# Layer 1 of a two-layer transformer kernel: the values of four heads by Strassen's seven products, with other homes for weights, queries and outputs

## What is computed

```
q = (x @ wq).reshape(B, S, 32, 192)[..., :128]
k = (x @ wkv)[..., :4096].reshape(B, S, 32, 128)
v = (x @ wkv)[..., 4096:8192].reshape(B, S, 32, 128)
probs = softmax(where(causal, q k^T * 192**-0.5, -1e30))
x = layernorm(x + (probs @ v).reshape(B, S, 4096) @ wo)
```

## Time and profile before

| | |
|---|---|
| time, median of 3 runs | 1414.67 us (1414.52 to 1414.96) |
| the profiled execution | 1416.18 us |
| its span, first to last instruction | 1414.4 us |
| TensorE busy | 1399.7 us (99%) |
| VectorE, ScalarE, GpSimd busy | 1015.6, 891.3, 773.7 us |
| layer 1's attention | from about 488 to 1340 us of the span |

### The profile page before, as it was taken

One profiled execution on the slowest core, in us unless ns is written; L12 is line 12 of the kernel. 1 busy time (PEld: TensorE's weight loads), 2 busy tenths in 40 slices (PEclk: granted clock), 3 DMA queues, 4 the chain that ended last, 5 costly groups with the idle time before them and its releaser, 6 DMA issues.

```text
span 1414.4 us, 30207 instructions
## 1 busy us (share of the span) xinstructions
PE 1399.7 (99%) x8769; PEld 1236.1 (87%) x8769; DVE 1015.6 (72%) x2528; ACT 891.3 (63%) x2445; POOL 773.7 (55%) x828
## 2 busy tenths in 40 slices
PE   9999999999999999999999999999999999999998
PEld 7898989888788888889889889889889889889886
DVE  5999999998968875665665665665665665665776
ACT  5888888888555576566566566566566556556721
POOL 3645555555040367765665665665665665665521
PEclk9999999999999999999999999999999999999999
DMA  5533333322445301111001002001001001000201
GB/s 197 164 100 89 101 89 100 89 73 50 129 139 155 107 31 46 46 31 59 30 30 59 30 30 59 30 30 59 30 30 59 30 30 59 30 30 30 83 20 42
DMA packets 56155, 92.60 MB, mean 65 GB/s; under 512 B 6064, under 2 KB 27312, under 8 KB 56112
## 3 DMA queue, kind: packets, MB, share of 16 engines
q1 hardware_dynamic: 55968, 91.93, 21.7%
q10 hardware_dynamic: 144, 0.13, 0.0%
HBM read 81.82 MB, written 2.10 MB: 59 GB/s over the span
## 4 chain that ended last, share of the span: by engine, by line
PE 93%; DVE 3%; ACT 2%; issue 1%; POOL 1%; DMA 0%; SPq 0%; POOLq 0%; DVEq 0%; ACTq 0%
PE c_bv L106 8%; PE c_bv L108 7%; PE c_bv L107 7%; PE h_bo L947 5%; PE c_bx L106 5%; PE c_bx L108 4%; PE c_bx L107 4%; PE c_by L106 4%; PE c_by L108 4%; PE c_by L107 4%; PE h_bo L1450 3%; PE a_acc L1450 3%; PE h_bt L75 3%; PE c_bt L75 2%; PE h_bs L106 2%; PE h_bs L108 2%
## 5 line engine op out<-in xcount | busy, mean ns | idle before, releaser
L621 POOL TENSOR_TENSOR h_pr<-h_pr,h_rinv 128x512 f32<-128x512 f32 x128 | 133.2, 1041 | 136.8 <-DVE h_rinv L772 134.5
L1781 POOL TENSOR_TENSOR c_qk<-g_y,c_qk 128x512 fp32r<-128x512 f32 x96 | 124.1, 1293 | 146.1 <-ACT c_qk L1893 139.3
L1632 POOL TENSOR_TENSOR b_sw_lo<-b_slots,b_sw_hi 128x512 fp32r<-128x512 f32 (+1 forms) x128 | 148.0, 1156 | 10.3
L1630 POOL CAST b_sw_hi<-b_slots 128x512 fp32r<-128x512 f32 (+1 forms) x128 | 72.7, 568 | 143.9 <-DMA b_slots<-in_w_qk 120.8
L106 PE MATMUL c_bv<-b_wv_hi,g_xT_hi 128*128 128x256 f32 x496 | 138.9, 280 | 0.2 <-DVE g_xT_lo L1186 0.2
L107 PE MATMUL c_bv<-b_wv_lo,g_xT_hi 128*128 128x256 f32 x496 | 138.8, 280 | 0.0
L108 PE MATMUL c_bv<-b_wv_hi,g_xT_lo 128*128 128x256 f32 x496 | 138.7, 280 | 0.0
L2002 DVE TENSOR_TENSOR c_bo<-c_bo,g_wo 128x128 f32<-128x128 f32 x128 | 38.3, 299 | 122.0 <-ACT g_wo L1868 117.5
L1893 ACT ACTIVATE c_qk<-g_y 128x512 fp32r<-128x512 f32 x96 | 60.7, 632 | 96.8 <-DVE g_y L2039 67.3
L674 ACT ACTIVATE h_pr<-h_bs,h_nmax 128x256 f32<-128x256 f32 x256 | 119.4, 480 | 2.5 <-DVE h_nmax L767 2.4
L1858 ACT ACTIVATE c_pr<-c_pr,c_rinv 128x128 f32<-128x128 f32 (+1 forms) x256 | 101.9, 448 | 9.0 <-DVE c_rinv L1992 9.0
(11 more groups left out here) (480 smaller groups left out, 5139.5 us busy)
## 6 DMA issues: line engine op xcount, KB each, us to landing
f_wi<-in_w_ffn SPq DMA_DIRECT2D x66, 256.0 KB, 2.7
b_slots<-in_w_qk SPq DMA_DIRECT2D x64, 256.0 KB, 3.0
a_w<-in_w_head SPq DMA_DIRECT2D x28, 352.0 KB, 2.9
h_part<-in_w_ffn SPq DMA_DIRECT2D x32, 264.0 KB, 2.8
b_raw_v<-in_w_v SPq DMA_DIRECT2D x16, 512.0 KB, 4.6
b_raw_o<-in_w_o SPq DMA_DIRECT2D x16, 512.0 KB, 4.5
h_o_mix<-h_o_hi SPq DMA_DIRECT2D x62, 128.0 KB, 2.2
b_ffn_w<-in_w_ffn SPq DMA_DIRECT2D x4, 576.0 KB, 5.5
```

Source lines behind the costliest of these rows:

```text
L621: pool.tensor_tensor(pr[b][:, :, :], pr[b][:, :, :], rinv[b][:, :][:, :, None].to_broadcast([P, 2, S]), ALU.mult)\
L1632: pool.tensor_tensor(self.sw[1][:, a:b], self.slots[:, a:b], f32(self.sw[0][:, a:b]), ALU.subtract)\
L1781: pool.tensor_tensor(lo, src, f32(hi), ALU.subtract).then_inc(s_sumlo, 1)
```

## The change

The unit of the loop is a quad `q` of four heads j with 16 steps u = 4j + t; quads 1 to 6 are the loop.

- Values of a quad are made by Strassen's scheme on two by two blocks: weights of 256 channels x 256 columns (two heads), tokens in halves of 512 and channels in halves of 256, worked on for one batch of each token half at a time ("pair" 0 and 1). `value_product` is 12 matmuls of 256 columns. The seven products v1 to v7 stand at u = 12 (v1, v2), 13 (v6, v5), 14 (v7), 15 (v4, v3) for pair 0; v1 of pair 1 comes at the end of u = 15, and v2, v6, v5, v7, v4, v3 at u = 0 to 2 of the quad itself. They gather in bv and a new bank bw. ScalarE copies bv (`value_copy`), VectorE adds bw (`value_total`), and four "corners" of v are split by ScalarE (`corner_hi`) and VectorE (`corner_lo`): 11, 22 and 12 from the summed copies in SBUF (`vy`), 21 from the bank bv. The first quad has straight values as before (`straight_batch`).
- GpSimd makes four sums of value weights per quad (`combine_v`, 128x512 each) and splits seven blocks (`split_v`) in place of 1024 columns per group.
- Outputs: one bank bo, so `values(s)` waits for `outs` of step s-1 (before: s-2). The outputs of heads go to three homes, and a fourth for the last head; the output weights lie in v's own home (even pairs) or in an unused part of xT (odd pairs). Tiles of the odd pair 2q-1 stand at u = 3 to 7 (2, 1, 2, 1, 2), of the even pair 2q at u = 8 to 11, and alternate between bv and bw.
- Queries and keys: one buffer. `sum_hi` 1 and 2 both stand at t = 2 (before: t = 1 and 2), and GpSimd's `rest` 1 and 2 follow split 2.
- SyncE loads the output weights when their home is free (`load_o`), the value weights of a quad in three transfers (`load_v`). The scratch that the program reserves for dynamic transfers is set to 256.

The diff, cut to its core:

```diff
+    def combine_v(self, pool, q):
+        lo, a21 = self.vraw[1], self.vraw[0][:, self.VS4, :]
+        def put(out, a, b, op):
+            pool.tensor_tensor(lo[:, out, :], a, b, op).then_inc(self.s_vhi, 1)
+        done = 11 * q - 9
+        pool.wait_ge(self.s_in["v"], 48 * q + 32)
+        put(self.VS1, a21, lo[:, self.VA22, :], ALU.add)
+        put(self.VS3, lo[:, self.VA11, :], a21, ALU.subtract)
+        pool.wait_ge(self.s_vhi, done + 1)
+        put(self.VS2, lo[:, self.VS1, :], lo[:, self.VA11, :], ALU.subtract)
+        pool.wait_ge(self.s_vhi, done + 3)
+        put(self.VS4, lo[:, self.VA12, :], lo[:, self.VS2, :], ALU.subtract)
+        pool.wait_ge(self.s_vhi, done + 4)
...
-        qk = [k.sb(f"qk{i}", [P, 2, 2, T], F32R) for i in range(2)]
...
+        qk = k.sb("qk", [P, 2, 2, T], F32R)
...
-        bo = [k.ps(f"bo{i}") for i in range(2)]
+        bw, bo = k.ps("bw"), k.ps("bo")
...
                 if now:
-                    rest(h + 1, 0, q0)
+                    rest(h + 1, 0)
                 if more and not entry:
                     self.combine(pool, h + 2)
-                if hd == 0 and has(gr + 1, NG):
-                    self.split(pool, "v", gr + 1, [(s_vmm, 4 * gr + 4)])
-                if hd == 1 and has(gr, NG - 1):
-                    if isinstance(gr, int) and gr == 0:
-                        pool.wait_ge(s_tslo, 4)
-                    self.split(pool, "o", gr, [(s_omm, 8 * gr)])
+                if ahead and j >= 2:
+                    for i in ((0, 1, 2), (5, 6))[j - 2]:
+                        self.split_v(pool, q + 1, i)
                 if more:
                     self.split_qk(pool, h + 2, 1, [(s_x, 4 * h + 6), (s_y, 3 * h + 4)])
+                    self.split_qk(pool, h + 2, 2, [(s_x, 4 * h + 7), (s_y, 3 * h + 5)])
+                if ahead and j == 2:
+                    for i in (3, 4):
+                        self.split_v(pool, q + 1, i)
                 if now:
-                    rest(h + 1, 1, k1)
-                if more:
-                    self.split_qk(pool, h + 2, 2, [(s_x, 4 * h + 7), (s_y, 3 * h + 5)])
-                if now:
-                    rest(h + 1, 2, q1)
+                    rest(h + 1, 1)
+                    rest(h + 1, 2)
                 if more:
                     self.split_qk(pool, h + 2, 3, [(s_x, 4 * h + 8), (s_y, 3 * h + 6)])
-                if hd == 0 and in_last(gr):
-                    self.split(pool, "o", gr, [(s_wlo, 4 * NH)])
+                if entry:
+                    return
+                if j == 1:
+                    self.split_o(pool, 2 * q, wo_homes[0])
+                    if ahead:
+                        self.combine_v(pool, q + 1)
+                if j == (2 if is_last(q) else 3):
+                    self.split_o(pool, 2 * q + 1, wo_homes[1])
...
+                    b = straight_batch(q, u - 1)
+                    if b is not None:
+                        value_hi(NB + b, 1, b, tile_bank(b))
+                    if filled and u == 0:
+                        value_copy(2 * q - 1, 0)
+                    if filled and u == 1:
+                        corner_hi(2 * q - 1, "11", 1)
+                    if filled and u == 2:
+                        value_copy(2 * q - 1, 2)
+                    if filling and u == 13:
+                        corner_hi(2 * q, "11", 0)
+                    if filling and u == 15:
+                        corner_hi(2 * q, "22", 0)
+                    probs(s)
                     if has(s - 1, NSTEP):
-                        outs(s - 1, hd if t else 1 - hd, (t - 1) % 4)
-                    keys_first = light(gr, hd) and t == 2
+                        outs(s - 1, out_region(h - 1 if t == 0 else h, (j - 1) % 4 if t == 0 else j), (t - 1) % 4)
+                    if filled and u == 0:
+                        corner_hi(2 * q - 2, "12", 0)
+                    if filled and u == 1:
+                        value_copy(2 * q - 1, 1)
+                    if filled and u == 3:
+                        corner_hi(2 * q - 1, "12", 1)
+                    keys_first = light(h) and t == 2
                     if keys_first:
-                        key_hi(h + 1, 1 - hd)
+                        key_hi(h + 1)
                     if has(s + 1, NSTEP):
                         exps(s + 1, (t + 1) % 4)
+                    if filling and u == 12:
+                        value_copy(2 * q, 0)
+                    if filling and u == 13:
+                        value_copy(2 * q, 1)
                     if t < 2 and has(h + 1, NH):
                         copy(h + 1, t + 1)
                     if t == 2 and has(h + 1, NH) and not keys_first:
-                        key_hi(h + 1, 1 - hd)
+                        key_hi(h + 1)
+                    if filling and u == 14:
+                        value_copy(2 * q, 2)
+                    if filling and u == 15:
+                        corner_hi(2 * q, "21", 0)
                     if has(s + 1, NSTEP):
                         normalise(s + 1, (t + 1) % 4)
                     if t == 3 and has(h + 2, NH):
                         copy(h + 2, 0)
-                    if t < 3 and has(h + 1, NH):
-                        sum_hi(h + 1, 1 - hd, t)
-                    if hd == 1 and in_last(gr):
+                    if t == 0 and has(h + 1, NH):
+                        sum_hi(h + 1, 0)
+                    if t == 2 and has(h + 1, NH):
+                        sum_hi(h + 1, 1)
+                        sum_hi(h + 1, 2)
+                    if filled and u == 2:
+                        corner_hi(2 * q - 1, "22", 1)
+                        corner_hi(2 * q - 1, "21", 1)
...
+                    b = straight_batch(q, u - 1)
+                    if b is not None:
+                        value_lo(NB + b, 1, b, tile_bank(b))
+                    if filled and u == 0:
+                        value_total(2 * q - 2, 2)
+                    if filled and u == 1:
+                        corner_lo(2 * q - 1, "11", 1)
+                    if filled and u == 3:
+                        value_total(2 * q - 1, 2)
+                    if filling and u == 13:
+                        corner_lo(2 * q, "11", 0)
+                    if filling and u == 15:
+                        corner_lo(2 * q, "22", 0)
                     if has(s + 1, NSTEP):
                         maxes(s + 1, (t + 1) % 4)
-                    few = light(gr, hd)
+                    few = light(h)
                     if few and t == 3:
                         probs(s)
                     if has(s - 1, NSTEP):
-                        outs(s - 1, hd if t else 1 - hd, (t - 1) % 4)
-                    if has(s, NSTEP) and not (few and t == 3):
+                        outs(s - 1, out_region(h - 1 if t == 0 else h, (j - 1) % 4 if t == 0 else j), (t - 1) % 4)
+                    if not (few and t == 3):
                         probs(s)
+                    if filled and u == 0:
+                        corner_lo(2 * q - 2, "12", 0)
+                    if filled and u == 3:
+                        corner_lo(2 * q - 1, "12", 1)
                     if few and t == 2:
-                        key_lo(h + 1, 1 - hd)
+                        key_lo(h + 1)
                     if has(s + 1, NSTEP):
                         inverse(s + 1, (t + 1) % 4)
-                    if hd == 0 and not in_last(gr) and has(gr - 1, NG):
-                        add_out(8 * (gr - 1) + 2 * t, 2 * t, bv)
+                    add(0)
+                    if filled and u == 2:
+                        value_total(2 * q - 1, 1)
                     if t == 2 and has(h + 1, NH) and not few:
-                        key_lo(h + 1, 1 - hd)
+                        key_lo(h + 1)
+                    if filled and u == 0:
+                        value_total(2 * q - 1, 0)
+                    if filling and u == 12:
+                        value_total(2 * q, 0)
                     if t < 3 and has(h + 1, NH):
                         total(h + 1, t)
-                    if hd == 0 and not in_last(gr) and has(gr - 1, NG):
-                        add_out(8 * (gr - 1) + 2 * t + 1, 2 * t + 1, bv if t < 3 else by)
-                    if in_last(gr):
-                        steps = last_steps.get((hd, t), ())
-                        if hd == 1 and t == 2:
+                    add(1)
+                    if filling and u == 14:
+                        value_total(2 * q, 1)
+                    if filling and u == 15:
+                        corner_lo(2 * q, "21", 0)
+                    if filled and u == 2:
+                        corner_lo(2 * q - 1, "22", 1)
+                        corner_lo(2 * q - 1, "21", 1)
...
+                def v1(to, pair):
+                    n = 2 * to - 2 + pair
+                    if pair:
+                        pe.wait_ge(s_clo, corners(n - 1, "21"))
+                    else:
+                        pe.wait_ge(s_oadd, 16 * to - 9)
```

(72 more changed lines are left out.)

504 lines of the change are left out of this document (311 added, 193 removed).

## The result

The median after is 1419.5 us (1417.87 to 1420.64, 7 runs), before in the same session 1414.96 us (1414.52 to 1416.15, 7 runs): a ratio of 1.0031, 95% interval 1.0021 to 1.0041. The profiled execution took 1418.15 us with a span of 1416.2, against 1416.18 and 1414.4.

What follows compares the result with a forecast made beforehand. TensorE was taken to bound layer 1 without waits; -19.9 us of matmuls plus 9.8, 7.7 and 2.0 us of new waits gave -0.4 us, so 1414.3 us. The range was 1403 to 1422 us, the forecast's own 1411 to 1418.

Steps and rivals of the forecast that it cites:

- What bounds the kernel, and the price of a product: TensorE bounds layer 1; 14 blocks of 12 matmuls replace 16 in seven quads, at 1.42 us each: 19.9 us saved.
- Rival 3: Something beside TensorE's work limits the loop, so time follows the new waits only: 1425 us and more; chance 0.04.
- (a): One bank for outputs: values waits for the split of the step before; nothing, up to 0.3 us in steps without tiles.
- (b): One buffer of queries and keys, sum_hi 1 and 2 both at t = 2: costs nothing.
- (f): GpSimd's added combinations and half-blocks: 81 us of about 104 per quad, a queue costing nothing, with 0.8 us cover.
- (g): Six more 512-column operations per quad on ScalarE and VectorE, 3.6 us, falling into idle time, and the loads: nothing.
- rival 2: GpSimd's queue arrives late at u = 12, 1.0 us in seven quads: 1421 us; chance 0.22.
- (c): Hand-over at u = 2 to 3: first output tile waits for corner_lo 21 of pair 1, 1.4 us in seven quads: 9.8 us.
- (d): Hand-over at u = 15: v1 of pair 1 waits for corner_lo 21 of pair 0, 1.1 us seven times: 7.7 us.
- (e): Even pair's first tile at u = 8 waits for split_o: 0.1 us in six quads, 1.4 in the first; together 2.0 us.
- The sum: -19.9 + 9.8 + 7.7 + 2.0 = -0.4 us, applied to the median of 1414.67 us: 1414.3 us.
- Rival 1: Cheap hand-overs: copies miss GpSimd's instructions, (c) and (d) cost 0.6 us each per quad: 1404.2 us; chance 0.36.

Runs made afterwards that it cites:

- Experiments 7 and 9: Changed kernel, three reorderings, corner 22 of pair 0 behind the jump, v7 of pair 0 multiplied twice: 1414.41 us; this with VectorE's loop written out: 1408.83 us.
- experiment 8: The kernel of experiment 4 with VectorE's loop over quads 1 to 6 written out: 1399.02 us, ratio 0.9888 to the kernel before.
- Experiment 1: Changed kernel with corner 21 of pair 1 put ahead of sum_hi 1 and corner 22 at u = 2: 1414.91 us, ratio 0.9996 to the kernel before.
- experiment 5: Changed kernel with GpSimd's rest 2 cut to 16 of 512 columns in the first of every four heads: 1418.71 us, ratio 1.0026 to the kernel before.
- experiment 2: Changed kernel with corner 22 of pair 0 moved behind corner 21, to the end of u = 15: 1413.66 us, ratio 0.9990 to the kernel before.
- experiment 4: Changed kernel with corner 21 of pair 1 first, corner 22 of pair 0 last, output weights split ahead of rest 1: 1402.35 us, ratio 0.9911 to before.

## Why the prediction was wrong, step by step

**What bounds the kernel, and the price of a product: right.** The pitch of the earlier trace rows held. Experiments 7 and 9 measure it at 5.62 to 7.04 us for 12 matmuls more, and the 19.9 us are seen nearly whole once the waits are gone: -17.7 us of span in experiment 8, with 7 x 0.19 us left at u = 3 and some 0.6 us in the first quad, 19.6 together. The Trainium skill's gap for an isolated matmul (TensorE: Matmul & The Clock Gate, Back-to-back issue gap) would have made the added product 12 x 0.109 = 1.31 us, as an estimate; the step grew by 1.42, and the row was the better price. Rival 3 falls with this.

**(a), (b), (f), (g) at nothing: right.** The steps without a named wait last as long as the earlier trace rows has them, 7.03 to 7.07 us for 7.05, and no other wait of TensorE's matmuls between 560 and 1340 us comes to over 0.3 us. (Three idle times of its weight load do, 1.9 and 0.6 us put down to "issue" and 0.5 behind VectorE, each once.) In quad 3 `rest` 2 is done at u = 12 +2.9 and ScalarE's copy starts at +3.9, and u = 12 and 13 take 7.06 and 7.03 us; so rival 2, GpSimd's queue, falls too.

**(c) 9.8 us: right, 9.0 measured.** u = 3 takes 6.93 us for about 5.65, 1.28 in seven quads. The walk of offsets holds within 0.1 us up to the corners: `sum_hi` 2 at +6.01, corner 22 on ScalarE at +6.55, `rest` 2 at +6.72, corner 22 on VectorE at +7.20. The stretched subtraction was expected to end at +8.6 and ended at +8.56. Experiment 1 takes the wait away and experiment 5 shows the exclusion.

**(d) 7.7 us: right in sum, 7.9 measured, in part by luck.** v1 was to be 1.1 us late. Against the 7.06 to 7.09 us of u = 15 without the wait (experiment 2) it is 0.8 in four quads, 1.4 to 1.9 in three. The 0.5 us "on average" for the lock was 0.35 in this execution, and nearly half of that hung on chance: in five quads the two instructions arrive within 0.01 us, with an outcome of 0 or 1.14 us, and in two the lock took 0.61 and 0.69. Experiment 1, where all seven went against VectorE, has 4.4 us more in the same place.

**(e) 2.0 us: this is the term that failed, 4.9 measured.** The chain was right (split 3, `split_o`, the first even tile) and its end was not. `rest` 2 was put at +6.7 of u = 6, where it stands when it is alone. With both `rest`s after the step's last `sum_hi`s, `rest` 1 began at +5.75 and `rest` 2 only behind it, at about +7.0. The low part was done at 883.20 - 869.51 = +13.7 instead of +13.4. TensorE, whose two steps took 5.56 + 5.53 us and not 5.6 + 5.6, came at 11.1 + 0.9 + 1.39 = +13.4 instead of +13.5. An error of 0.3 us and one of 0.1, on a hand-over that was put at 0.1 us; 0.48 came of it in six quads, and 2.0 instead of 1.4 in the first. (That 1.4 doesn't follow from the offsets that the prediction gives: with steps of 4.3 and 4.1 us TensorE comes at 4.3 + 4.1 + 0.9 + 1.39 = +10.7, 2.7 us ahead of +13.4.) The bound given for (e), 4 us, was passed.

**The sum.** The three terms are 9.0 + 7.9 + 4.9 = 21.8 us against 19.5, so the balance is 21.8 - 19.9 = +1.9 instead of -0.4; the profiled execution shows +1.97, the span +1.8. The median is 4.5 us above that of before, because the profiled execution of the changed kernel lay 1.4 us under its own median, while that of before lay 1.2 above (1416.18 against 1414.96). That is the second step that failed: the prediction took the difference between two profiled executions for that between the medians, on a kernel where a tie decides over some 1.1 us in each of five quads. That the ties make up the 2.6 us between the two is not shown. Both together, 2.3 us of terms ((c) 0.8 less, (d) 0.2 and (e) 2.9 more) and 2.6 of this, make the way from "no change" to "slower by 0.3%".

**Rival 1 (cheap hand-overs, 1404.2 us) was wrong for this order, and right as a view of what the change can be.** Its condition, that the hand-overs miss GpSimd's instructions, wasn't met by the order in which corners 22 and 21 stand. With another order (experiment 4) the kernel came out 2 us below that, and with VectorE's loop written out 5.

The Trainium skill's rule (SBUF — State Buffer, SBUF: two separate sides) that the pair of ports is an exclusive lock, for a VectorE instruction with two SBUF inputs against a GpSimd instruction that reads SBUF, whichever starts first, is borne out by these traces in both directions (1.36 and 1.83 us on VectorE, 1.83 us on GpSimd), and a cast of one operand is such an instruction too (0.93 us). The Trainium skill says that the other blocks for the whole instruction; the rows have it 0.15 us less.

What stays open: which of the two engines wins a tie at the same hundredth, and why the idle time at a jump back varies (1.40 to 2.57 us). Unrolling the other engines' loops wasn't tried.

## What to carry to other kernels

When a change replaces work on a saturated engine by sums and copies on others, price the hand-overs by walking the queue of each engine, and put what nobody waits for (here corner 22) behind what the bound engine waits for (corner 21). A margin of a tenth of a microsecond on such a walk is smaller than the walk's own error (0.3 us here), and is to be priced by that error, not by its middle. The end of a loop's body is not free either: the last instruction ahead of a jump back should be early, or the loop of that engine written out.
